# Two of sixteen C products of a Mamba slot with time on the partitions, and new orders for the slot

## The reference, cut to what matters

```
xz = x @ in_w.T ; xm, z = split(xz)
xm = silu(causal_conv(xm) + cb)                # 4 taps, 256 inner channels
dt, Bm, Cm = split(xm @ xp_w.T, [8, 8+16])     # 16 states
dt = softplus(dt @ dt_w.T + dt_b)
dA = exp(dt[..., None] * A)
dBu = dt[..., None] * Bm[:, :, None, :] * xm[..., None]
h[l] = dA[l] * h[l-1] + dBu[l]                 # scan over time
y = einsum('blds,bls->bld', h, Cm) + xm * D_skip
out = (y * silu(z)) @ out_w.T
```

## Time and profile before

| | us |
|---|---|
| median of 3 runs (1296.54 to 1297.84) | 1297.77 |
| the profiled execution's own time | 1294.75 |
| its span in the trace | 1292.9 |
| slots 1 to 13 in the trace (87.6 to 734.0) | 646.4 |
| slots 14 and 15 (734.0 to 834.2) | 100.2 |

### The profile page before, as it was taken

The page is one execution under the profiler, slowest core; times in us unless marked ns, Lnnn a source line. Parts: engine busy times, 40 slices in busy tenths (PEclk is TensorE's granted clock), DMA queues, the critical chain, the costliest instruction groups (busy, mean ns, idle before and its releaser), DMA issues.

```text
span 1292.9 us, 22737 instructions
## 1 busy us (share of the span) xinstructions
PE 1223.2 (95%) x6828; PEld 688.0 (53%) x6829; DVE 1125.9 (87%) x1639; ACT 1016.9 (79%) x2563; POOL 1099.0 (85%) x642
## 2 busy tenths in 40 slices
...
GB/s 203 246 252 153 157 242 151 198 215 124 222 237 91 253 224 68 278 194 108 271 171 126 243 150 241 120 145 59 98 75 51 26 14 27 27 22 15 10 10 14
DMA packets 49590, 178.84 MB, mean 138 GB/s; under 512 B 15672, under 2 KB 33500, under 8 KB 40924
## 3 DMA queue, kind: packets, MB, share of 16 engines
...
## 4 chain that ended last, share of the span: by engine, by line
PE 38%; DVE 27%; issue 18%; ACT 12%; POOL 4%; DMA 1%; DVEq 1%; another core or an unknown queue 0%; SPq 0%; ACTq 0%; POOLq 0%
DVE h L1616 19%; PE banks L306 10%; DVE h L1597 6%; PE banks L483 5%; ACT banks L1578 5%; PE banks L878 4%; PE banks L983 3%; POOL h L1622 3%; PE banks L494 3%; PE banks L926 3%; PE banks L1657 2%; ACT L1449 2%; ACT xm L1412 1%; ACT L1446 1%; PE banks L1405 1%
## 5 line engine op out<-in xcount | busy, mean ns | idle before, releaser
L1622 POOL TENSOR_TENSOR h<-h,Cb 128x1024 f32<-128x1024 f32 (+2 forms) x166 | 582.4, 3544 | 10.7 <-DVE h L1616 10.2
L1616 DVE TENSOR_TENSOR_SCAN h<-banks,h 128x1024 f32<-128x1024 f32 x256 | 569.0, 2274 | 1.8 <-ACT banks L1578 0.4
L1578 ACT ACTIVATE banks<-dt,A_cur 128x255 f32<-128x255 f32 x1024 | 424.2, 462 | 73.3 <-DVE h L1616 70.1
L1657 PE MATMUL banks<-h,ident 128*128 128x512 f32 x1016 | 469.0, 601 | 4.3 <-DVE yz L1676 2.2
L1657 PEld LDWEIGHTS banks<-h,ident 128*128 128x128 f32 x1016 | 185.8, 190 | 238.5 <-issue 197.7
L1597 DVE TENSOR_TENSOR h<-Bb,banks 128x1024 f32<-128x1024 f32 (+2 forms) x101 | 200.2, 1999 | 1.3 <-ACT banks L1562 0.7
L1603 POOL TENSOR_TENSOR h<-Bb,u 128x1024 f32<-128x1024 f32 (+1 forms) x50 | 184.1, 3683 | 1.9 <-DVE xs L1519 1.8
L919 POOL TENSOR_SCALAR Cb<-Cb,h 128x128 f32<-128x128 f32 x124 | 96.4, 798 | 32.9 <-DVE h L901 32.6
L1405 PE MATMUL banks<-xn,wF 128*128 128x512 f32 x256 | 113.0, 592 | 2.2 <-ACT xn L1397 2.2
L919 POOL TENSOR_SCALAR h<-h 128x128 f32<-128x128 f32 x124 | 92.5, 762 | 16.2 <-DVE h L901 15.8
L1405 PEld LDWEIGHTS banks<-xn,wF 128*128 128x128 f32 x256 | 47.4, 188 | 63.5 <-issue 60.3
...
...
## 6 DMA issues: line engine op xcount, KB each, us to landing
Cb<-scrX SPq DMA_DIRECT2D x32, 2048.0 KB, 8.9
Bb<-scrX SPq DMA_DIRECT2D x31, 2048.0 KB, 12.5
...
h<-in_L_ffn_w SPq DMA_DIRECT2D x2, 2048.0 KB, 8.7
...
```

The source lines that it names most:

```text
L1578: m = e.activation(ps_dA[c % 2][:, g, half, 1:S], dts[q][:, half, i * S + 1:(i + 1) * S], ACT.Exp, scale=A_cur[q][:, s:s + 1])
L1616: e.tensor_tensor_scan(chunk(i, c), ps_dA_flat[c % 2], chunk(i, c), 0.0, ALU.mult, ALU.add).then_inc(sem("scan"), 1)
L1622: e.tensor_tensor(h[i][:, rows(cs), :, :], h[i][:, rows(cs), :, :], both(Cb[i], cs), ALU.mult).then_inc(sem("hC"), len(cs))
L1657: m = e.matmul(bank(5), ident[:], h_flat[i][:, s * HALVES * S:(s + 1) * HALVES * S], start=(s == GROUP * first_sum(p, i)), stop=(s == NS - 1))
```

## The change

In slots 1 to 13 chunks 2 and 4 of sequence b no longer get their C product on POOL. For each of their four states, PE turns the scanned state so that time lies on the partitions (`hT`: four transposes of 128x128 into bank 4 for chunk 2, bank 7 for chunk 4). ACT scales it from there back into h with a column of C as its per-partition scale (`hT`: two instructions of 256 columns). PE turns it back as transposes that add into bank 5 (`yT`: four for each state). For the columns, PE turns C of sequence b (`turnC`: four matmuls of 16 columns from 32 rows of `xd`) and ACT copies them (`turnC`). In these slots POOL also makes the B product of chunk b5, which DVE made before. One silu phase takes the place of two, and the four lists are new. Waits come in: `back` waits until the last scaled state of the slot before is made, `ucopy:n` for the last one in bank 4. Products are counted by slot now, since the share of POOL differs between slots.

The diff, cut:

```diff
-POOL_MUL = ((4, 5, 6), (6, 7))
-DVE_MUL = tuple(tuple(c for c in range(CHUNKS) if c not in pool) for pool in POOL_MUL)
+POOL_EDGE = ((4, 5, 6), (6, 7))
+POOL_STEADY = ((4, 5, 6), (5, 6, 7))
+TURNED = ((), (2, 4))
+TURN_BANK = {(1, 2): (4, 4), (1, 4): (7, 7)}
+TURNS = [(i, c, g) for i in range(2) for c in TURNED[i] for g in range(GROUP)]
+TURN_STEPS = 1 + len(TURNS)
+LAST_IN_4 = max([0] + [k + 1 for k, (i, c, g) in enumerate(TURNS) if TURN_BANK[i, c][g] == 4])
+TURN_FROM = 0 if TURNED[0] else 1
+TURN_COLS = 2 * (2 - TURN_FROM)
 FC_TAP = 0
...
+def steady(p):
+    return not isinstance(p, int) or 1 <= p <= SLOTS - 3
+
...
+def turn_step(p, k):
+    return TURN_STEPS * (p - 1) + k + 1
+
+
+LAPS = 1 + NPAIR
...
         def pe_back(e, t, q):
             e.wait_ge(sem("xg"), t + 1)
+            if steady(t - 2 if isinstance(t, int) else t):
+                e.wait_ge(sem("scaled"), LAPS + turn_step(t - 2, TURN_STEPS - 1))
...
         def act_ucopy(e, p, q, i):
             e.wait_ge(sem("u"), i + 1 if isinstance(p, int) and p == 0 else 2 * p + 2)
-            wait(e, sem("mulv"), products(DVE_MUL, p, i))
+            wait(e, sem("mulv"), products(dve_mul_of, p, i))
+            if i == 0 and steady(p - 1):
+                e.wait_ge(sem("scaled"), LAPS + turn_step(p - 1, LAST_IN_4))
...
             e.tensor_tensor(h[i][:, rows(cs), :, :], h[i][:, rows(cs), :, :], both(Cb[i], cs), ALU.mult
-                            ).then_inc(sem("hC"), len(cs))
+                            ).then_inc(sem("hC"), len(cs) + (turned_ahead(i, cs[0]) if steady(p) else 0))
...
+        def turned_state(i, c, g, a):
+            at = (GROUP * c + g) * HALVES * S + a * HALVES * P
+            return h_flat[i][:, at:at + HALVES * P]
+
+        def pe_turnC(e, p, q, i):
+            e.wait_ge(sem("xd"), p + 1)
+            e.wait_ge(sem("mulv"), products(dve_mul_of, p, i) + len(dve_mul_of(p)[i]))
+            for k in range(TURN_COLS):
+                at = TURN_FROM * S + k * P
+                m = e.matmul(bank(4)[:, k * NS:(k + 1) * NS], xd[q][0:BC, at:at + P], ident[0:BC, NS:BC],
+                             start=True, stop=True)
+            m.then_inc(sem("lap"), 1)
+
+        def act_turnC(e, p, q, i):
+            e.wait_ge(sem("lap"), LAPS + turn_step(p, 0))
+            e.activation(CT, fold(bank(4)[:, 0:TURN_COLS * NS], TURN_COLS), ACT.Copy).then_inc(sem("scaled"), 1)
+
+        def pe_hT(e, p, q, i, c, g):
+            k = 1 + TURNS.index((i, c, g))
+            at = TURN_BANK[i, c][g]
+            e.wait_ge(sem("scan"), CHUNKS * (2 * p + i) + c + 1)
+            if at == 7:
+                e.wait_ge(sem("dt"), p + 3)
+            if same_bank(k):
+                e.wait_ge(sem("scaled"), LAPS + turn_step(p, same_bank(k) - 1))
+            for a in range(2):
+                for half in range(HALVES):
+                    col = (GROUP * c + g) * HALVES * S + half * S + a * P
+                    m = e.transpose(bank(at)[:, (a * HALVES + half) * P:(a * HALVES + half + 1) * P],
+                                    h_flat[i][:, col:col + P], ident[:])
+            m.then_inc(sem("lap"), 1)
+
+        def act_hT(e, p, q, i, c, g):
+            k = 1 + TURNS.index((i, c, g))
+            e.wait_ge(sem("lap"), LAPS + turn_step(p, k))
+            for a in range(2):
+                m = e.activation(turned_state(i, c, g, a), bank(TURN_BANK[i, c][g])[:, a * HALVES * P:(a + 1) * HALVES * P],
+                                 ACT.Identity, scale=CT[:, 2 * (i - TURN_FROM) + a, GROUP * c + g:GROUP * c + g + 1])
+            m.then_inc(sem("scaled"), 1)
+
+        def pe_yT(e, p, q, i, c, g):
+            k = 1 + TURNS.index((i, c, g))
+            e.wait_ge(sem("scaled"), LAPS + turn_step(p, k))
+            for a in range(2):
+                for half in range(HALVES):
+                    at = half * S + a * P
+                    e.matmul(bank(5)[:, at:at + P], turned_state(i, c, g, a)[:, half * P:(half + 1) * P], ident[:],
+                             start=False, stop=False, is_transpose=True)
...
 PE_ORDER = """
-back sum:l6 conv:0 conv:1 sum:l7 z:0 out z:1 sum:a0 sum:a1 sum:a2 sum:a3 xproj sum:a4 dt:0 dt:1 sum:a5 sum:a6 sum:a7
-+center sum:b0 sum:b1 sum:b2 sum:b3 sum:b4 sum:b5"""
+sum:l6 back sum:l7 conv:0 conv:1 out z:0 z:1 xproj sum:a0 turnC:b dt:0 dt:1 sum:a1 sum:a2 sum:a3 sum:a4 sum:a5 hT:b20
+sum:a6 hT:b21 sum:a7 +center hT:b40 sum:b0 hT:b41 sum:b1 sum:b3 sum:b5 yT:b20 yT:b21 yT:b40 yT:b41"""
 ACT_ORDER = """
-xn dA:a2 dA:a3 dA:a4 silus xm:0 xm:1 exps dA:a5 dA:a6 ucopy:b res dA:a7 dA:b0 silus zs:0 zs:1 exps dA:b1 xd dA:b2
-dA:b3 sp_abs sp_exp sp_ln dA:b4 dA:b5 +square dA:b6 dA:b7 +lnv ucopy:n +rstd +scale dA:n0 dA:n1"""
+xn dA:a2 dA:a3 dA:a4 dA:a5 ucopy:b silus xm:0 xm:1 res zs:0 zs:1 exps dA:a6 xd dA:a7 turnC:b dA:b0 sp_abs dA:b1 dA:b2
+sp_exp sp_ln dA:b3 hT:b20 dA:b4 hT:b21 dA:b5 dA:b6 hT:b40 dA:b7 hT:b41 ucopy:n +square +lnv dA:n0 +rstd dA:n1 +scale"""
 DVE_ORDER = """
-mul:a01 mul:a2 scan:a0 scan:a1 scan:a2 mul:a3 scan:a3 scan:a4 gate:l mul:a7 scan:a5 scan:a6 mul:b012 scan:a7 scan:b0
-scan:b1 mul:b345 scan:b2 scan:b3 dt gate:a scan:b4 scan:b5 scan:b6 scan:b7"""
+mul:a01 mul:a2 mul:a3 mul:a7 scan:a0 scan:a1 scan:a2 scan:a3 gate:l scan:a4 mul:b012 mul:b34 scan:a5 scan:a6 scan:a7
+scan:b0 scan:b1 scan:b2 dt scan:b3 scan:b4 gate:a scan:b5 scan:b6 scan:b7"""
 POOL_ORDER = """
-C:l7 mul:a456 C:a012 mul:b6 C:a3 C:a45 C:a67 mul:b7 C:b01 C:b23 C:b4 u C:b5 C:b6"""
+C:l7 mul:a456 mul:b5 C:a012 C:a3 mul:b6 C:a45 C:a67 C:b01 mul:b7 u C:b3 C:b5 C:b6"""
 PE_OPEN = """
 lap:1 center lap:2 back lap:3 conv:0 conv:1 z:0 sum:a0 sum:a1 z:1 sum:a2 xproj sum:a3 dt:0 sum:a4 dt:1 sum:a5 sum:a6
 sum:a7 sum:b0 sum:b1 +center sum:b2 sum:b3 sum:b4 sum:b5"""

```

More of the change, by code:

```diff
@@ L81, with pool_mul_of, dve_mul_of, products @@
 SC_END = SC_OUT + HALVES * P
-def products(table, p, i):
-    return (len(table[0]) + len(table[1])) * p + (len(table[0]) if i else 0)
+def steady(p):
+    return not isinstance(p, int) or 1 <= p <= SLOTS - 3
+def pool_mul_of(p):
+    return POOL_STEADY if steady(p) else POOL_EDGE
+def dve_mul_of(p):
+    return tuple(tuple(c for c in range(CHUNKS) if c not in pool) for pool in pool_mul_of(p))
+def products(share, p, i):
+    before = lambda k: sum(len(cs) for cs in share(k))
+    if isinstance(p, int):
+        return sum(before(k) for k in range(p)) + (len(share(p)[0]) if i else 0)
+    return (p - 1) * before(1) + before(0) + (len(share(p)[0]) if i else 0)
+def turned_ahead(i, c):
+    n = 0
+    while c - n - 1 in TURNED[i]:
+        n += 1
+    return n
+def same_bank(k):
+    banks = [4] + [TURN_BANK[i, c][g] for i, c, g in TURNS]
+    return max([j + 1 for j in range(k) if banks[j] == banks[k]], default=0)
+def turn_step(p, k):
+    return TURN_STEPS * (p - 1) + k + 1
+LAPS = 1 + NPAIR
 LN_AFTER = 4
@@ L160, in program @@
         xc = sb("xc", [P, PAIR])
+        CT = sb("CT", [P, TURN_COLS, NS])[:]
         yz = sb("yz", [P, HALVES, 2, S])
@@ L335, in muls_done @@
             def muls_done(p, i):
-                e.wait_ge(sem("mulv"), products(DVE_MUL, p, i))
-                e.wait_ge(sem("mulp"), products(POOL_MUL, p, i))
+                e.wait_ge(sem("mulv"), products(dve_mul_of, p, i))
+                e.wait_ge(sem("mulp"), products(pool_mul_of, p, i))
             def second_weight(b):
@@ L352, in tail_sync @@
             e.wait_ge(sem("ub"), 2 * LAST)
-            e.wait_ge(sem("mulp"), products(POOL_MUL, LAST, 0))
+            e.wait_ge(sem("mulp"), products(pool_mul_of, LAST, 0))
             second_weight(2)
@@ L1298, in spread_B @@
             def spread_B(t, i):
-                wait(e, sem("mulv"), products(DVE_MUL, t - 1, i) + len(DVE_MUL[i]) if t else 0)
-                wait(e, sem("mulp"), products(POOL_MUL, t - 1, i) + len(POOL_MUL[i]) if t else 0)
+                wait(e, sem("mulv"), products(dve_mul_of, t - 1, i) + len(dve_mul_of(t - 1)[i]) if t else 0)
+                wait(e, sem("mulp"), products(pool_mul_of, t - 1, i) + len(pool_mul_of(t - 1)[i]) if t else 0)
                 if t == 0 and i == 0:
@@ L1593, in dve_mul @@
         def dve_mul(e, p, q, i, *cs):
-            if cs[0] == DVE_MUL[i][0]:
+            if cs[0] == dve_mul_of(p)[i][0]:
                 e.wait_ge(sem("ub"), 2 * p + i + 1)
@@ L1807, in act_gelu @@
             if b == 1:
-                e.wait_ge(sem("mulv"), products(DVE_MUL, LAST, 1))
-                e.wait_ge(sem("mulp"), products(POOL_MUL, LAST, 1))
+                e.wait_ge(sem("mulv"), products(dve_mul_of, LAST, 1))
+                e.wait_ge(sem("mulp"), products(pool_mul_of, LAST, 1))
             wait(e, sem("dn"), b - 1)
```

24 lines of the change are left out of this document (13 added, 11 removed).

## The result

The kernel after takes 1280.62 us (median of 4 runs, 1278.62 to 1281.51) beside 1297.45 us for the one before (4 runs, 1296.54 to 1297.84): ratio 0.9869, interval 0.9851 to 0.9887. It is faster by 16.8 us, and by more than I forecast: 1287.5, with a range from 1282.5 on. The profiled execution took 1278.62 us with a span of 1276.8, that is 16.1 less than the span before.

A forecast was written before the change was run, and what follows sets the result against it. DVE and POOL were taken to bound a slot together. Slot 48.6 + 0.3 = 48.9, 0.83 less, x 13 = 10.8, less 0.5 for slot 14: 10.3 off 1297.77 gives 1287.5 us; 8-in-10 range 1282.5 to 1297.

The forecast's parts named there:

- What bounds the kernel: Slots 1 to 13: DVE and POOL bound a 49.73 us slot together; relief of one alone would give nothing.
- 48.6 + 0.3 for the two places = 48.9: New slot: DVE's 48.6 us plus 0.3 idle where PE or ACT may come late; 0.83 less than before.
- The work, 48.6: DVE in a slot: 49.73 less 1.06 for chunk b5 gives 48.7; a drain saved 0.1 to 0.2 more.
- The layout by hand: New order of a slot, each instruction starting when engine and inputs are ready, plus 0.05 for the semaphore; ends at 48.4.
- The idle time, 0.3: DVE waits in a slot, at gate:a for PE and ahead of scans b3 and b4 for ACT: 0.3 us together.
- Place one: PE up to gate:a: one unbroken row ends at 41.5, DVE is there at 41.3, so 0.2 to 0.3 idle.
- place two: ACT from dA:b2 to dA:b5: 10.2 us against DVE's 10.5, 0.3 to spare, entered late by about that.
- first rival: Full gain: PE and ACT come in time at both places, drains vanish; slot 48.5, 1282 us; chance 0.13.
- POOL's bracket ahead of C:a45: POOL in a slot: one wait of about 1 us ahead of C:a45, released by a scan.
- rival 3: PE's transposes with bare weight loads, 0.25 each, make PE set the slot: 1310 to 1326 us; chance 0.08.
- rival 2: PE or ACT late, zero slack at both places: slot 49.2 to 49.6, 1291.5 to 1297 us; chance 0.19.
- Rival 4: PE's clock falls around transposes, 3.4 us at half clock setting PE back 1.7: 1309 us; chance 0.04.

The follow-up runs named there:

- the second try at a third chunk: Kernel after, with chunk b5 turned too, b4's B product also on POOL and lists laid out anew: 1278.5 us, ratio 0.9891 to the kernel before.

## Why the prediction was too cautious, by its own steps

**What bounds the kernel** was right. b5 back on DVE costs 1.07 of the 1.06 that I gave a chunk, and without the turns POOL sets the slot at 51.78. Relief of POOL alone, with the new orders, gives 0.14 a slot; relief of DVE alone, with them, costs 2.06. Both engines had to be relieved together.

**The step that failed is the base of "48.6 + 0.3 for the two places = 48.9".** Measured, from the start of each instruction to that of the next (mean of slots 2 to 12): 48.28 of work on DVE and 0.24 of short waits. The work was mis-sized by 0.3, the waits by less than 0.1.

- *The work, 48.6.* I took the measured slot of 49.73 as work on DVE, less 1.06 for b5 and 0.1 for a drain. Those two are about right (1.05, and 0.10 to 0.13). But the measured slot was not all work. It held some 0.3 us of short waits that show no bracket, because the tail of the instruction before covers them. In slot 7 of the kernel before:

```profile
402.03 1.21 DVE L1597 TENSOR_TENSOR h<-Bb,banks 128x1024 f32<-128x1024 f32 x1
403.29 4.47 DVE L1616 TENSOR_TENSOR_SCAN h<-banks,h 128x1024 f32<-128x1024 f32 x2
...
435.70 2.29 DVE L1597 TENSOR_TENSOR h<-Bb,banks 128x2048 f32<-128x2048 f32 x1
```

The multiplication of a7, whose product scan a5 behind it does not read, takes 1.26 to the next start (402.03 to 403.29) where such a one takes 1.13 without a wait. The last four scans take 8.87 up to the next slot's first multiplication (426.83 to 435.70) where four take 8.74 in the kernel after (385.13 to 393.87). With the slower restart behind each, the two waits are 0.14 each in the mean, and the new orders have neither. "No idle bracket on either" was rightly read and wrongly taken to mean no idle time.
- *The layout by hand* is made of durations laid end to end, has no such waits in it, and was right to 0.1 all along: scans a0 to a3 end at 14.4 (measured 14.3), scans to b2 at 35.8 (35.7), gate:a at 41.3 (41.35), end 48.4 (48.5). With my own 0.3 of idle time on it the slot would have been 48.7.
- *The idle time, 0.3.* It came out at 0.24: 0.06 at scan b1, 0.15 at scan b4, 0.03 at gate:a, ACT's part being the larger. Place one had PE at y of a at 41.5; it came at 41.31. I charged `turnC` as 4 matmuls of 16 columns and 0.9 us. That was a reading error, in the description of the change too: TURN_COLS is 2 x (2 - TURN_FROM) = 2, so it is two matmuls and a copy of 32 columns. `turnC` with dt takes 1.92 where I charged 0.9 + 1.7 = 2.6; the kernel that does have four takes 2.38. The error matters little, because PE's row up to the gate is not unbroken as I had it: `hT:b20` waits 0.22 for scan b2, so PE's work ahead of it could be that much longer or any amount shorter, and the gate would stand where it stands. At place two the scalings took 0.36 each where I took 0.40.

So the likeliest case was in truth my first rival, the full gain (slot 48.5, 1282 us), to which I gave 0.13. Its slot came out to 0.01, which is partly luck: not all waits at the two places vanished, and what it had not counted, the waits of the old slot, made up for them. The 0.39 a slot by which 48.9 was too high is 5.1 of the 6.9 us between 1287.5 and 1280.62. Most of the rest is slot 15, 1.65 us shorter without the clock fall that before's trace has there; what decides whether the clock falls in it I did not find out.

**What else held.** POOL's bracket ahead of C:a45 is 0.82 for about 1. Slot 14 lost 0.4 for 0.5. Transposes stand 0.11 apart (16 in 1.91 with tail, 32 in 3.50), their weight loads hidden, so rival 3 was wrong. mul:b5 never waits for its load in slots 1 to 13. "Zero slack at both places", for which I gave rival 2 its 0.19, is shown for the chain behind scan b2: eight more transposes are paid whole. Ahead of scan b2 PE has 0.22 in hand. Zero slack is not a loss, though. PE comes 0.04 before it is wanted.

**The clock.** Rival 4, which the prediction also calls the last one, did not happen in the change, but its price for PE was right: each fall in the kernel with four matmuls in `turnC` costs 1.7. The cause that I named, transposes, was not seen. The Trainium skill (TensorE: Matmul & The Clock Gate, Part 4: PE-mode transpose) says that transposes do not count as activity for the clock; this case's trace does not agree: 3.50 us of nothing but transposes, thirteen times over, left the granted clock at 1.00, the 2.4 GHz level, in every slot. A longer row wasn't tried. The falls that I looked at in the two kernels without turns follow a PE with much idle time, as in the earlier trace rows. In the one with the orders alone, by stretch:

```profile
431.10:434.50 3.40, 1.38 (x10) 1.01 (x9) 3.40 (x4) 2.82 (x7) 3.40 (x2) 1.00 0.67 231
434.50:437.90 3.40, 3.40 (x6) 1.69 (x5) 3.40 (x2) 2.29 (x7) 3.40 (x2) 0.51 0.92 386
```

PE was busy 1.38 of 3.40 us and then ran at 0.51. Those with four matmuls in `turnC` follow a stretch of small matmuls in which PE shows busy throughout, and those in the second try at a third chunk follow one with only the two matmuls of the kernel after and PE busy 3.25 to 3.34 of 3.40. So the number of these matmuls alone does not decide it. Which property does wasn't tried.

**The orders** I had judged as harmless in themselves. They cost 0.93 a slot without the turns. The sum did not suffer from this, because the new orders were made and laid out together with the turns, but costing the parts one by one would have gone wrong by that much.
